# First edge of equal nodes found by a weight column in the merging matmul of a graph layer

## What is computed

```python
s = s @ W_nl0;  v = einsum('nmi,mk->nki', v, W_nl1)
w = relu(edge_feature @ W_fc1) @ W_fc2            # 224 weights of an edge
xs, xv = s[dst], v[dst]                           # gather by node
tp = concat([w0*xs, w3*dot(xv, sh1), w1*xs*sh1, w2*xv, w4*cross(xv, sh1)])
agg = segment_sum(tp, src, num_segments=N) / 32   # scatter by node
out_s = agg_s @ W_out_s + skip_s;  out_v = agg_v W_out_v + skip_v
x = x + concat([silu(out_s[:, :64]), sigmoid(out_s[:, 64:]) * out_v])
```

## Time and profile before

| what | value |
|---|---|
| median of 3 runs | 1385.2 us (1382.02 to 1385.59) |
| the profiled execution | 1387.66 us, its span 1385.8 us |
| POOL busy | 1066.5 us (77%) |
| PE busy | 919.5 us (66%) |
| DVE busy | 880.1 us (64%) |
| ACT busy | 428.5 us (31%) |
| granted PE clock, mean | 0.78 |

### The profile page before, as it was taken

How to read it: one execution, slowest core, us unless ns; L and a number is a source line. 1 busy time by engine, 2 the same in 40 slices (tenths; PEclk the granted TensorE clock), 3 DMA queues, 4 the chain that set the end, 5 groups by cost and what they waited for, 6 DMA issues and landing times.

```text
span 1385.8 us, 26047 instructions
## 1 busy us (share of the span) xinstructions
PE 919.5 (66%) x5648; PEld 780.3 (56%) x5648; DVE 880.1 (64%) x3693; ACT 428.5 (31%) x839; POOL 1066.5 (77%) x830
## 2 busy tenths in 40 slices
PE   7498766757757768577677675776766757769103
PEld 5387655646646657466566574665655646658102
DVE  7899747657566576575675766656647667579105
ACT  5154332322323323223233232232332323325101
POOL 1777788888888888888878888788788887887880
PEclk9699877786877877778778787787787877779556
DMA  9635555555454555554555555545554555456557
GB/s 351 165 92 102 105 80 86 99 80 105 81 80 105 78 84 101 80 105 80 80 105 80 88 97 81 104 79 82 105 78 88 97 80 106 79 78 90 52 55 274
DMA packets 124075, 139.89 MB, mean 101 GB/s; under 512 B 34241, under 2 KB 99585, under 8 KB 123970
## 3 DMA queue, kind: packets, MB, share of 16 engines
q0 software_dynamic: 79296, 74.04, 38.2%
q1 hardware_dynamic: 44674, 64.92, 15.1%
HBM read 86.24 MB, written 52.66 MB: 100 GB/s over the span
## 4 chain that ended last, share of the span: by engine, by line
DMA 31%; POOL 26%; DVE 23%; issue 14%; PE 3%; DVEq 2%; ACT 0%; POOLq 0%; SPq 0%; ACTq 0%
DMA sums<-to_add,add_idx 15%; DMA sums<-spare,add_idx 15%; POOL turn_space L388 9%; POOL sums L406 8%; DVE products_space L805 6%; POOL rows L388 5%; POOL spare L388 5%; DVE products_space L834 4%; DVE before L873 2%; DVE same L872 2%; DVE products_space L832 2%; DVE products_space L831 2%; DVE radial L847 1%; DVE msg L858 1%; DVE turn_space L816 1%
## 5 line engine op out<-in xcount | busy, mean ns | idle before, releaser
L507 PE MATMUL t_ps<-w,products_space 128*128 128x128 f32 (+1 forms) x1248 | 225.2, 312 | 350.6 <-DVE products_space L834 350.6
L523 PEld LDWEIGHTS o_ps<-w,pT 128*128 128x128 f32 (+1 forms) x2496 | 360.5, 223 | 40.7 <-issue 37.9
L406 POOL DMA_INDIRECT sums<-to_add,add_idx x208 | 326.6, 1570 | 67.9 <-issue 47.3
L507 PEld LDWEIGHTS t_ps<-w,products_space 128*128 128x128 f32 (+1 forms) x1248 | 166.3, 160 | 373.7 <-issue 335.8
L523 PE MATMUL o_ps<-w,pT 128*128 128x96 f32 (+1 forms) x2496 | 376.6, 309 | 0.0
L406 POOL DMA_INDIRECT sums<-spare,add_idx x208 | 326.6, 1570 | 64.4 <-issue 46.0
L631 ACT ACTIVATE pT<-t_ps 128x512 f32<-128x512 f32 (+1 forms) x312 | 185.4, 594 | 320.2 <-PE t_ps L507 319.7
L897 DVE TENSOR_TENSOR add_idx<-key,from_col 128x4 int32<-128x4 f32 x104 | 16.9, 163 | 371.0 <-DMA sums<-spare,add_idx 206.7
L388 POOL DMA_INDIRECT turn_space<-node_table,to_idx x186 | 187.1, 1006 | 56.7 <-issue 46.7
L640 ACT ACTIVATE msg<-o_ps 128x448 f32<-128x448 f32 x208 | 113.0, 543 | 335.8 <-PE o_ps L523 327.4
L538 PE MATMUL d_ps<-msg,same 128*128 128x192 f32 x832 | 197.0, 365 | 28.4 <-ACT spare L652 20.6
(11 more groups left out here) (96 smaller groups left out, 865.6 us busy)
## 6 DMA issues: line engine op xcount, KB each, us to landing
from_row<-nodes_row SPq DMA_DIRECT2D x52, 512.0 KB
ef<-edge_t SPq DMA_DIRECT2D x52, 256.0 KB
turn_space<-node_table SPq DMA_DIRECT2D x768, 0.6 KB
spare<-node_table SPq DMA_DIRECT2D x768, 0.6 KB
turn_space<-sums SPq DMA_DIRECT2D x9, 480.0 KB, 7.0
sums<-zeros SPq DMA_DIRECT2D x6, 672.0 KB, 9.2
sums<-to_add,add_idx POOLq DMA_INDIRECT x208, 3.6
sums<-spare,add_idx POOLq DMA_INDIRECT x208, 3.6
```

Of the source, the lines that this page charges most:

```text
L406: pool.indirect_dma_start(sums[t], bass.IndirectOffsetOnAxis(ap=add_idx[:, 2 * v + h, j:j + 1], axis=0), to_add[2 * v + h][:, j, :], None, ...
L507: ins = nc.tensor.transpose(t_ps[(3 * u + c) % 2][0:ROWS[c], j * P:(j + 1) * P], prod[:, u % 2, j, a:e], ident)
L523: ins = nc.tensor.matmul(o_ps[m][:, base + oc:base + oc + n], pT[c][u % 2][:, cols], w[0:ROWS[c], wc:wc + n], start=(q == 0 and c == 0), s ...
```

## The change

The weights' constant block loses the triangle `lower` and gains two columns: a rank of each partition, 3 to the power 63 - p, and twice that rank. The message ring `msg` becomes `ranked`, with the rank as a column ahead of each message row, so that the merging matmul (193 columns in place of 192) also sums the ranks of the equal nodes. Powers of 3 are so far apart that this sum is at most twice an edge's own rank just where no earlier edge has its node. ACT copies 193 columns to `to_add`, whose rows are now 208 values apart, the sum at value 16 of each and the rank ahead of it. L873 and its accumulator read go. The rule "is the sum at most twice my rank" is now a small DVE operation on ACT's copy (`repeats`), which waits for `sums_ready`, in DVE's step g + 4 and between `same_nodes` and `radial_part`, and the index is made after it in the same step (`rows_to_add`), without a wait for landings. The two indices ahead of the loop now come inside it. SP's load of block b + 1 waits for the matrices `same` of the groups up to 2b - 1 and, for b above 4, explicitly for the landing of all scatters of block b - 5.

```diff
--- before.py
+++ after.py
@@ -60,9 +60,10 @@
 W_MA = W_FC2 + 2 * S + 3 * V
 W_MB = W_MA + SO
 W_MC = W_MB + 3 * V
-W_LT = W_MC + 3 * V
-W_DUMP = W_LT + P
-W_END = W_DUMP + 1
+W_DUMP = W_MC + 3 * V
+W_RANK = W_DUMP + 1
+W_FIRST = W_RANK + 1
+W_END = W_FIRST + 1
 NA = W_NC - W_NA
 NODE_SKIP, NODE_ROWS = 2 * V, 2 * V + SO
 NFC2 = 2 * S + 3 * V
@@ -83,6 +84,8 @@
 ROWS_PER_BLOCK = P * len(BY_ROW_SLOTS) // (ROWS_RING // 2)
 ROWS_PER_LOAD = 16
 EARLY_GROUPS = 2
+SUM_AT = 16
+SUM_ROW = SUM_AT + M
 AHEAD = 7
 SKEW = 3
 LOOP = RING // 2
@@ -160,12 +163,11 @@
 
         w = sb("w", [P, W_END])
         ident = w[:, W_ID:W_ID + P]
-        lower = w[:, W_LT:W_LT + P]
         x_sb = sb("x_sb", [P, NT, F])
         turn_space = sb("turn_space", [P, NT * F + NT * 2 * P])
         h_quads = [turn_space[:, tt.start * F:tt.stop * F].rearrange("p (f t) -> p f t", t=tt.stop - tt.start)
                    for tt in QUADS]
-        spare = sb("spare", [P, max(NT * (S + M + 3 * V), UNROLL * J * (G_END + M))])
+        spare = sb("spare", [P, max(NT * (S + M + 3 * V), UNROLL * J * (G_END + SUM_ROW))])
         node_out = spare[:, 0:NT * (S + M + 3 * V)].rearrange("p (t f) -> p t f", t=NT)
         bn = sb("bn", [P, NT, 6])
         mean_var = sb("mean_var", [P, NT, 2])
@@ -191,19 +193,19 @@
         crs = products_space[:, 0:3 * J * 3 * V].rearrange("p (n j f) -> p n j f", n=3, j=J)
         prod = products_space[:, 3 * J * 3 * V:].rearrange("p (k j f) -> p k j f", k=2, j=J)
         pT = [[sb(f"pT{c}{k}", [ROWS[c], GE]) for k in range(2)] for c in range(3)]
-        msg = sb("msg", [P, 2, J, OUTS])
+        ranked = sb("ranked", [P, 2, J, 1 + OUTS])
+        msg = ranked[:, :, :, 1:1 + OUTS]
         radial = sb("radial", [P, 2, 2, 3 * V])
         same = sb("same", [P, 2, J, P])
-        before = sb("before", [P, J, P])
-        key = sb("key", [P, 3, 2, J])
-        to_add_0 = sb("to_add_0", [P, UNROLL, J, M])
-        to_add_1 = spare[:, UNROLL * J * G_END:UNROLL * J * (G_END + M)].rearrange(
+        key = sb("key", [P, 2, UNROLL, J])
+        to_add_0 = sb("to_add_0", [P, UNROLL, J, SUM_ROW])
+        to_add_1 = spare[:, UNROLL * J * G_END:UNROLL * J * (G_END + SUM_ROW)].rearrange(
             "p (u j m) -> p u j m", u=UNROLL, j=J)
         to_add = [(to_add_0, to_add_1)[r // UNROLL][:, r % UNROLL] for r in range(RING)]
         add_idx = sb("add_idx", [P, RING, J], I32)
 
 
-        vec = msg[:, :, :, :].rearrange("p k j f -> p (k j f)")[:, 0:3 * TILES].rearrange("p (t i) -> p t i", i=3)
+        vec = ranked[:, :, :, :].rearrange("p k j f -> p (k j f)")[:, 0:3 * TILES].rearrange("p (t i) -> p t i", i=3)
         vlen = to_add_0[:, :, :, :].rearrange("p u j m -> p (u j m)")[:, 0:5 * TILES].rearrange("p (k t) -> p k t", k=5)
 
         hid_ps = ps("hid_ps", [P, GE])
@@ -284,7 +286,7 @@
             def load_from(b, par):
 
                 if valid(b - 2, BLOCKS):
-                    sp.wait_ge(idx_ready, 2 * b - 2)
+                    sp.wait_ge(same_ready, 2 * b - 2)
                 sp.dma_start(from_col[:, par, :], nodes_from[:, bass.ds(b * 2 * J, 2 * J)]).then_inc(from_in[par], 16)
                 sp.dma_start(from_row[:, par, :],
                              nodes_row[:, bass.ds(b * 2 * GE, 2 * GE)].partition_broadcast(P)
@@ -332,7 +334,14 @@
             sp.wait_ge(by_row_in, 16)
             sp.wait_ge(table_out, 16 * STEPS)
             sp.wait_ge(skip_out, 16 * 3)
+            def scatters_landed(b):
+
+                for t in range(TABLES):
+                    sp.wait_ge(added[t], 16 * scattered(t, b, 2 * J))
+
             for b in range(BLOCKS):
+                if b + 1 < BLOCKS and b > LOOP:
+                    scatters_landed(b - LOOP - 1)
                 if b + 1 < BLOCKS:
                     load_from(b + 1, (b + 1) % 2)
                 if b + 2 < BLOCKS:
@@ -405,7 +414,7 @@
                             pool.wait_ge(added[t], 16 * scattered(t, b, p))
                         pool.indirect_dma_start(
                             sums[t], bass.IndirectOffsetOnAxis(ap=add_idx[:, 2 * v + h, j:j + 1], axis=0),
-                            to_add[2 * v + h][:, j, :], None, compute_op=ALU.add,
+                            to_add[2 * v + h][:, j, SUM_AT:SUM_ROW], None, compute_op=ALU.add,
                         ).then_inc(added[t], 16)
 
             pool.wait_ge(to_in, 16)
@@ -535,8 +544,8 @@
                 if valid(g - 1, GROUPS) or m == 1:
                     pe.wait_ge(sums_ready, 2 * g + m)
                 for q in range(2):
-                    ins = nc.tensor.matmul(d_ps[:, q * M:(q + 1) * M], same[:, u % 2, 2 * m + q, :],
-                                           msg[:, u % 2, 2 * m + q, 0:M], start=(q == 0), stop=(q == 1),
+                    ins = nc.tensor.matmul(d_ps[:, q * (1 + M):(q + 1) * (1 + M)], same[:, u % 2, 2 * m + q, :],
+                                           ranked[:, u % 2, 2 * m + q, 0:1 + M], start=(q == 0), stop=(q == 1),
                                            skip_group_check=True)
                 ins.then_inc(summed, 1)
 
@@ -649,8 +658,8 @@
                     for j in (2 * m, 2 * m + 1):
                         t, n = landed(b - LOOP, u, j)
                         act.wait_ge(added[t], n)
-                nc.scalar.activation(to_add[u][:, 2 * m:2 * m + 2, :],
-                                     d_ps[:, 0:2 * M].rearrange("p (q o) -> p q o", q=2),
+                nc.scalar.activation(to_add[u][:, 2 * m:2 * m + 2, SUM_AT - 1:SUM_ROW],
+                                     d_ps[:, 0:2 * (1 + M)].rearrange("p (q o) -> p q o", q=2),
                                      ACT.Copy).then_inc(sums_ready, 1)
 
             def step(i, u):
@@ -783,6 +792,8 @@
                                                   vlen[:, 3, :].unsqueeze(2).broadcast_to([P, TILES, n]), ALU.mult)
                 ins.then_inc(rhat_ready, 1)
                 dve.wait_ge(rhat_ready, 1)
+                nc.vector.tensor_scalar(ranked[:, :, :, 0], w[:, W_RANK:W_RANK + 1].unsqueeze(2).broadcast_to([P, 2, J]),
+                                        1.0, None, ALU.mult)
 
             def vecs(ap, n):
                 return ap.rearrange("p j (i k) -> p j i k", i=n)
@@ -865,41 +876,35 @@
                 dve.wait_ge(from_in[par], 32 * (2 * i + u // 4 + 1))
                 if valid(g - 2, GROUPS):
                     dve.wait_ge(summed, 2 * g - 2)
-                    dve.wait_ge(idx_ready, g - 1)
+                if valid(g - UNROLL, GROUPS):
+                    dve.wait_ge(repeats_ready, g - UNROLL + 1)
                 for j in range(J):
-                    row = from_row[:, par, (h * J + j) * P:(h * J + j + 1) * P]
-                    col = from_col[:, par, h * J + j:h * J + j + 1]
-                    nc.vector.tensor_scalar(same[:, k, j, :], row, col, None, ALU.is_equal)
-                    nc.vector.scalar_tensor_tensor(before[:, j, :], row, col, lower, ALU.is_equal, ALU.mult,
-                                                   accum_out=key[:, 0, k, j:j + 1])
-
-                nc.vector.tensor_scalar(key[:, 1, k, :], from_col[:, par, h * J:(h + 1) * J], -1.0,
+                    nc.vector.tensor_scalar(same[:, k, j, :], from_row[:, par, (h * J + j) * P:(h * J + j + 1) * P],
+                                            from_col[:, par, h * J + j:h * J + j + 1], None, ALU.is_equal)
+
+                nc.vector.tensor_scalar(key[:, 0, u % UNROLL, :], from_col[:, par, h * J:(h + 1) * J], -1.0,
                                         w[:, W_DUMP:W_DUMP + 1], ALU.mult, ALU.add).then_inc(same_ready, 1)
 
             def repeats(g, u):
-                if not valid(g, GROUPS):
-                    return
-                k = u % 2
-                dve.wait_ge(same_ready, g + 1)
-                nc.vector.scalar_tensor_tensor(key[:, 2, k, :], key[:, 0, k, :], 0.5, key[:, 1, k, :],
-                                               ALU.is_gt, ALU.mult).then_inc(repeats_ready, 1)
-
-            def rows_to_add(g, u, b):
-
-                if not valid(g, GROUPS):
-                    return
-                par, h, k = u // 2 % 2, u % 2, u % 2
+
+                if not valid(g, GROUPS):
+                    return
+                dve.wait_ge(sums_ready, 2 * g + 2)
+                nc.vector.scalar_tensor_tensor(key[:, 1, u % UNROLL, :], to_add[u][:, :, SUM_AT - 1],
+                                               w[:, W_FIRST:W_FIRST + 1], key[:, 0, u % UNROLL, :],
+                                               ALU.is_le, ALU.mult).then_inc(repeats_ready, 1)
+
+            def rows_to_add(g, u):
+
+                if not valid(g, GROUPS):
+                    return
                 dve.wait_ge(repeats_ready, g + 1)
-                if valid(g - RING, GROUPS):
-                    for j in range(J - TABLES, J):
-                        t, n = landed(b - LOOP, u, j)
-                        dve.wait_ge(added[t], n)
```

(31 more changed lines are left out.)

## The result

The changed kernel takes 1396.1 us (median of 6 runs, 1390.7 to 1398.9), the kernel before 1384.8 us over the runs beside it: a ratio of 1.0077, 95% interval 1.0061 to 1.0094. The forecast was 1384.5 us, no change. The kernel became 11 us slower, beyond the range, and the change did what it says.

A forecast was written before the change was run, and what follows sets the result against it. POOL's issue rate was taken as the bound from 36 to 1352 us. All terms were 0 except -1 us for shorter POOL instructions: 1387.66 to 1386.7 profiled, 1384.2 as median, given as 1384.5, range 1378 to 1391.

The forecast's parts named there:

- The triangle comparison: L873 on DVE goes: 83 to 112 us less DVE busy time, 0 on the path.
- The rank column: One more column in PE's merging matmul and ACT's copy: 1.6 us of PE, under 3 ns a copy, path 0.
- the new source rows: Scatter source rows in `to_add` 208 values apart instead of 192, same bytes a row: 0.
- SP's wait: SP's block load waits directly for landings and can start 0.6 us earlier: value 0, bounds -3 and +3.
- the late index: DVE makes the index behind ACT's copy in step g + 4, still eight groups ahead of its use: path 0.
- POOL's instructions get shorter?: POOL's gathers and scatters, with DVE doing less beside them: between 0 and 27 us gained, taken as 1 us.
- These waits cost nothing: DVE's 371.0 us idle before L897 and ACT's copy wait for landings eight groups back: a full ring's brake, no cost.
- None of the three: Besides the slower and faster rivals, a third: index later than POOL wants it, time over 1395, chance 0.02.
- The slower one, landings beyond the turn: Scatter landings over 5.6 us make POOL wait twice a block; 0.1 us beyond costs 10 us: 1396, chance 0.10.
- The faster one: POOL freed of DVE: removing L873, with two SBUF inputs, returns 4 to 14 us, some 1375; chance 0.13.

The follow-up runs named there:

- the last runs: Changed kernel with all large two-input DVE instructions made one-input reductions, 1365.7 us; cross products as 12 one-input multiplications there, 1378.6, with DVE's landing wait, 1403.6, in the kernel before, 1407.7.
- all one input: Changed kernel with cross products, their difference, the radial part and its addition made one-input reductions, that computation left out: 1365.7 us (0.9844 to 0.9877).
- three versions with the new cross products: Cross products as 12 one-input multiplications, difference in three instructions: on the changed kernel 1378.6 us, with DVE's landing wait put back 1403.6, in the kernel before 1407.7.

## Why the prediction was wrong

- **The bound was right.** POOL's issue rate sets the time from 36 us to the last scatter, and the span less POOL's instructions is 323 us within 3 in every kernel above.
- **The costs put at nothing were nothing by themselves.** The triangle comparison freed 106 us of DVE (83 to 112 foreseen) and gave no time: with DVE let go at the old place the time is 1.0000 of the old one. The rank column, the new source rows (landings still 3.6 us), SP's wait and the late index cost nothing that the runs could show. POOL never waited long for a sum or an index: its idle time ended by ACT in front of scatters is 3.4 us in three waits, the longest 1.7.
- **The step that failed is "POOL's instructions get shorter?".** It saw the excess, put it at 27 us, and bounded the change's part between 0 and all of it gone. The term stood in the sum at -1 us and measured +13.4 (1073.6 for 1060.2). It asked only what the removed instruction would give back. The excess belongs to the meetings of POOL's starts with the other two-input instructions of DVE, and a change that moves DVE against POOL can raise it: from 22 us over the undisturbed lengths before to 36 after (both worked out from the traces in the same way). There had to be a bound on the loss side, and the last runs show how far it goes: 1082.9 - 1040.7 = 42 us between the best and the worst.
- **The row chosen to settle it was the wrong one.** I took the gather from 80.20 at 0.96 us to show that L873 doesn't harm POOL, and let it stand for DVE as a whole. It shows neither. The L873 under it had begun only 0.05 us earlier, and one that begins within 0.07 us of POOL's start adds nothing (42 starts of the kernel before, 0.1 us in all). One that began 0.08 us earlier added 0.14 us to the gather from 372.55 (timeline of the kernel before; an undisturbed gather takes 0.95):

```profile
80.15 0.37 DVE L873 SCALAR_TENSOR_TENSOR before<-from_row,from_col,w 128x128 f32<-128x128 int32 x1
...
372.47 0.34 DVE L873 SCALAR_TENSOR_TENSOR before<-from_row,from_col,w 128x128 f32<-128x128 int32 x1
372.55 1.09 POOL L388 DMA_INDIRECT rows<-node_table,to_idx  x1 [0.30 <-issue]
```

L873 follows the same rule as the other two-input instructions, but at 0.34 us it leaves little: 157 of POOL's starts in the kernel before fell into one, for 2.4 us in all, while 91 starts in the cross products cost 11 us. So removing it gave back about 2 us, and the others took some 15 us more. The right rows were the long gathers themselves, each with what DVE ran at its start.

- **The rule of the Trainium skill was the answer, and I took its wrong half.** SBUF — State Buffer, "Who interferes with whom", says that a VectorE instruction with two SBUF inputs keeps GpSimd from reading SBUF until it ends, and infers that descriptor generation isn't touched. An indirect DMA's instruction is given its row numbers in SBUF, here `to_idx` and `add_idx`. The runs agree with the first half (all one input: -30 us). For indirect DMAs they do not agree with what the inference leads to, that a `tensor_tensor` leaves POOL alone. That it is the reading of these row numbers that waits is argued and not shown.
- **"These waits cost nothing" was true and not enough.** DVE's 371 us of idle time had no price, but the wait set the moment of each DVE instruction against POOL's starts. I also named the wrong place of the new one: DVE doesn't stand at `repeats` (9.1 us) but at the radial part, 434.9 us, because ACT's order puts the wait for the landing ahead of the copy of the messages.
- **The rivals.** None of the three occurred. The slower one, landings beyond the turn, would show 5 us of landing; they are at 3.6. The faster one had the right mechanism, but L873 had little to give back, and the move of the other instructions gave the change its sign.

What stays open: the alignment doesn't seem to be fixed by the program alone (one execution of six in the run with SP's old wait took the short one, and it alone has a trace), and I could not tell ahead which alignment an edit gives; of three versions with the new cross products one gained and two lost. Nor did I find what decides, where two-input instructions follow one another without a gap, whether the lengthening ends with the one under way (230 of 247 starts under cross products with over 0.12 us of one left) or runs on to the last (most starts under the three short differences). Why the first two instructions of each POOL run are longer (1.62 and 1.58 us for scatters, also without any two-input neighbour) is open too.

## What to carry to other kernels

When GpSimd writes indirect-DMA descriptors back to back, count VectorE's `tensor_tensor` instructions with two SBUF inputs, and in a smaller measure its `tensor_scalar`, as a load on GpSimd: look at the lengths of its instructions one by one, beside what VectorE runs at their starts, and give such instructions one SBUF input where it can be done (with the other input in PSUM they cost nothing here, as `tensor_scalar` a little). When a wait is moved, even one that costs nothing, ask what it keeps in step: here it set which VectorE instruction was under way at each start on the bounding engine. With the kind of these instructions, that made the kernels with the whole computation differ from the kernel before by -6 to +22 us. A forecast of such a kernel needs a range on both sides of zero as wide as the whole excess that the trace shows.

## What was new about the hardware

- A POOL indirect DMA that starts under a DVE `tensor_tensor` or `scalar_tensor_tensor` with two SBUF inputs is longer by what is left of that one, less 0.125 us (238 starts over all traces, each within 0.02 us). Nothing is added where the DVE instruction has under 0.12 us left or begins behind POOL's start, and under L873 nothing either where it began within 0.07 us of it (other kinds lengthen it from some 0.03 us on).
- Where such instructions follow one another without a gap, the lengthening mostly ends with the one under way, but it can run on: 1.92 us for 1.56 under three short differences.
- A `tensor_tensor` with one input in PSUM and a reduction add nothing (0.000 and 0.001 us over 363 and 429 starts). With all large two-input instructions gone the mean scatter is 1.566 us.
- A `tensor_scalar` with one large SBUF input does add something: 0.06 us in the mean under 128 values, 0.03 under 96. Its time also grows by half as much for each value as a reduction's: from one to the next it is 0.18 us at 96 values and 0.20 at 128, against 0.19 at 128 and 0.33 at 256 for the reduction. Whether the two belong together is not shown.
- The cross products as 12 `tensor_scalar` of 96 values take 2.35 us, against 1.6 us for the five two-input products of the same group: DVE did 80 us more work and the kernel was 17 us faster.
